# A two-layer transformer on one core: where the softmax maxima of both attentions are split into bf16 parts and turned

## The chip, the core and the metric

The kernel runs on one core of one Trainium2 chip. A core has engines that run side by side, each with its own list of instructions: TensorE (PE in the profile; its weight loads are shown apart, as PEld), VectorE (DVE), ScalarE (ACT), GpSimd (POOL) and SyncE (SP), which issues most of the DMAs. Work reaches TensorE from on-chip SBUF and leaves it in the eight banks of PSUM. Engines wait for each other on semaphores. The metric is the time of one execution on the device in microseconds (us), the median of several; lower is better.

## What is computed

Tokens `x` of shape 8 x 512 x 128 go through four stages, each added to its input: an attention with rotary embedding and a small feed-forward (layer 0), 16 experts of which each token takes two, a causal attention with an extra bias (layer 1), and 8 experts of which each token takes two. The change touches the two attentions. Cut to what matters:

```python
# layer 0, 16 heads of 8 columns
q, k, v = x_norm @ Wq + bq, x_norm @ Wk + bk, x_norm @ Wv + bv
scores = einsum('bhqd,bhkd->bhqk', rope(q) / sqrt(hd), rope(k))
out = softmax(scores) @ v
# layer 1, 16 heads of 8 columns, causal
logits = einsum('bhqd,bhkd->bhqk', q, k) * scale + incidence * decay**(q_pos - k_pos) * bias_scale
attn = softmax(where(causal_mask, -inf, logits))
out = einsum('bhqk,bhkd->bqhd', attn, v)
```

The softmax needs the maximum of each row of logits (one for each token and head) before the exponential is taken.

## The kernel before, in words

**Both attentions** work batch by batch (8 batches of 512 tokens, T = 4 tiles of P = 128 tokens) and in quads of QUAD = 4 heads, so 4 quads a batch and 32 quads in an attention. Each batch of logits is made twice. The first time it stands with the queries on the partitions, so VectorE can take the maximum along a row; the second time it stands transposed, with the keys on the partitions, and there ScalarE takes the exponential. In the transposed form the maximum belongs to a column, so it has to be turned (from 128 tokens x 4 heads to 4 rows x 512 tokens) and subtracted by TensorE as extra rows of the contraction. For that it is held as two bf16 parts, the high part of minus the maximum and what is left.

The step in question, in both attentions, for one quad before the change:

1. VectorE's maxima of the quad are complete (`maxed`; in layer 1 after `join`, L1870, which gives `mjoined`).
2. TensorE: `turn_max` turns the four tiles by fp32 transposes into the PSUM bank `TB` (L1124, L2042).
3. ScalarE: `minus_max` copies `-TB` to bf16, the high part (L808, L1695).
4. VectorE: `minus_max` reads `TB` and the high part and writes the low part (4 rows x 512; L949, L1874). On VectorE's list it stands after further maxima.
5. The two parts reach the product. In layer 0 by two DMAs on SyncE into the rows `STACK` of `QS` (L658, `mstacked`). In layer 1 directly: the matmul of `pick` and `less` (L2049 in `diagonal`, L2054 in `below`) adds them to the scores.
6. `scores(i, g, 0)` of the quad on TensorE waits for `mstacked` (layer 0) or for `mhigh` and `mlow` (layer 1).

**The order on each engine** is written out by hand. In layer 0 a quad has 8 units `j`; in unit `j` TensorE runs `scores(i, g, j)` (L1156), at `j == 5` the `turn_max` of the next quad, then the logits of a head 12 units ahead (L1116), parts of `values` (L1135) and small pieces of other batches. VectorE runs two maxima (L944) per unit, `attend` (L955, L959) at `j == 4`, `minus_max` at `j == 5`.

In layer 1 TensorE runs, for a quad, four times `scores(i, g, j)`, pieces of other batches and `logits` of the next quad's head `j + 1`; then `scores(i, g, 4)`, `values(.., 0)`, `turn_max` of the next quad and `values` 1 to 3, and then the first `scores` of the next quad. `logits` is the product of the incidence (L2016, 54 rows contracted), the diagonal blocks (L2022, L2023) and the blocks of the past (L2028 to L2034). VectorE takes them with `maxima` (L1849, L1854, L1855, L1857, L1862, L1865). Its list at the end of a quad is: `join` of the next quad, `maxima` of one head of the quad after it, `minus_max`, then `attend` of this quad (L1881, L1885), which waits until TensorE has turned the values (L2103). In `scores(i, g, j)` with `j < 4` the products are, in order: L2048 (transposed diagonal), L2049, L2054, L2055, L2048, L2049, L2054, L2055, L2048, L2049; in `scores(i, g, 4)` they are four times L2048, L2049, L2054, L2055.

`less` is 128 rows x 2 x 512 in bf16 before, zero but for rows 0 to 3 (high) and 32 to 35 (low); `pick` is 128 rows x 4 x 128 and selects a head's rows.

In the built program each matmul carries the size of the array tile that it uses: the contracted rows rounded up to 32, 64 or 128, and the columns of the stationary operand likewise. Before, L2016 carries 64 x 128 (54 rows), the products of `values` (L1135, L2093) carry 128 x 32, and nearly all others 128 x 128. A quad takes about 20 us in layer 1 (634 us for 32) and 17.5 us in layer 0 (560 us for 32).

## Time and profile before

| | us |
|---|---|
| median of 3 runs | 1950.77 |
| lowest, highest | 1941.09, 1951.09 |
| profiled execution, its own time | 1956.3 |
| its span, first to last instruction | 1954.6 |
| attention of layer 0, main part | 90 to 650 |
| attention of layer 1, main part | 1032 to 1666 |

Over the whole span PE is busy 77%, DVE 65%, ACT 46%, POOL 35%. The rows that the prediction rests on stand below. In a timeline a row gives the start, the length, the engine, the line, the operation, out<-in with the shapes, how many in a row (x4), and in brackets how long the engine sat idle before it and what ended that. Matmuls overlap: each lasts some 0.2 us, but the next starts well before that, so the price of one is the distance between two starts. A row of several (x2) spans from the first start to the last end.

### The profile page before, as it was taken

Reading aid. Unit: us, or ns where it says so; the run is one execution under the profiler, and the core shown is the slowest. Engines: PE = TensorE matmul, PEld = TensorE weight load, DVE = VectorE, ACT = ScalarE, POOL = GpSimd, SP = SyncE. Lnnn points to the kernel's source line nnn. Section 1 sums busy time; section 2 is a strip of 40 time slices with the busy share of each in tenths; the row PEclk is TensorE's granted clock in tenths of the full one; section 3 lists DMA queues with packets and bytes.
Section 4 is the critical chain, followed back from the end, with each engine's and each line's share of the span. In section 5 each row is a group of like instructions: output and inputs, shape, how many; then the busy total and the mean of one; then the engine's idle time right before and its main releaser. Section 6 shows DMA issues by size and latency. Waiting matters only on the chain. (4 is left out here: it accounts for less than half of the span.)

```text
span 1954.6 us, 37276 instructions
## 1 busy us (share of the span) xinstructions
PE 1498.3 (77%) x11726; PEld 965.0 (49%) x11726; DVE 1274.9 (65%) x3485; ACT 891.8 (46%) x1807; POOL 681.0 (35%) x774
## 2 busy tenths in 40 slices
PE   1699999999999735996248979889798878325993
PEld 0123333333333325996125656666566655224993
DVE  1577888888888413555427777787777775553555
ACT  0156666666666502653334444554445534102661
POOL 1311223323321232553434333343334400475552
PEclk9998999999999957998659999999999999556997
DMA  4211112111111321224052444434444340411225
GB/s 110 65 42 54 38 46 60 47 49 59 47 49 31 118 105 41 72 71 117 27 173 82 133 119 139 119 108 132 121 131 122 111 132 11 127 47 55 72 73 148
DMA packets 121617, 166.36 MB, mean 85 GB/s; under 512 B 21458, under 2 KB 94962, under 8 KB 120786
## 3 DMA queue, kind: packets, MB, share of 16 engines
q1 hardware_dynamic: 112530, 145.69, 26.0%
q0 software_dynamic: 8896, 18.30, 2.7%
q8 instruction: 99, 1.62, 0.4%
q14 instruction: 92, 0.75, 0.1%
HBM read 116.04 MB, written 47.60 MB: 84 GB/s over the span
## 5 line engine op out<-in xcount | busy, mean ns | idle before, releaser
L944 DVE TENSOR_REDUCE a_M<-a_F 128x1 f32<-128x512 f32 x512 | 326.0, 680 | 59.8 <-PE a_F L1116 57.6
L841 ACT ACTIVATE L_W<-a_ST 128x512 f32<-128x512 f32 x512 | 277.2, 595 | 141.4 <-PE a_ST L1156 138.3
L1742 ACT ACTIVATE c_PT<-c_ST 128x1024 f32<-128x1024 f32 x160 | 163.4, 1021 | 201.0 <-PE c_ST L2049 155.3
L1156 PE MATMUL a_ST<-L_W 74*128 74x512 bf16 x512 | 170.8, 397 | 16.7 <-ACT L_W L841 7.2
L1116 PE MATMUL a_F<-L_W 72*128 72x512 bf16 x512 | 168.4, 404 | 13.4 <-DVE a_M L944 13.3
L2048 PE MATMUL c_ST<-ident,c_SD 128*128 128x128 f32 x512 | 145.7, 285 | 25.1 <-issue 17.3
L1135 PE MATMUL a_PV<-L_W,a_V 128*32 128x512 f32 x1024 | 141.1, 625 | 1.0 <-ACT L_W L841 1.0
L2275 ACT ACTIVATE L_hT<-L_P,L_W1s 128x128 f32<-128x128 f32 x316 | 90.6, 369 | 99.0 <-PE L_P L2403 58.3
L1849 DVE TENSOR_TENSOR c_inc<-c_INC,c_table 128x512 f32<-128x512 f32 x128 | 87.5, 684 | 55.5 <-PE c_INC L2016 46.5
L1156 PEld LDWEIGHTS a_ST<-L_W 74*128 74x128 bf16 x512 | 44.6, 99 | 149.4 <-ACT L_W L841 90.7
L2263 POOL DMA_INDIRECT L_yd<-L_ys,L_di x79 | 85.5, 1083 | 91.0 <-DVE L_ys L2348 89.1
L2049 PE MATMUL c_ST<-c_less,c_pick 128*128 128x128 bf16 x512 | 114.0, 223 | 0.0
L2659 ACT ACTIVATE L_hT<-L_P,L_W1s 128x128 f32<-128x128 f32 x284 | 81.4, 369 | 70.6 <-PE L_P L2917 52.3
L2055 PE MATMUL c_ST<-c_QS,c_KS 126*128 126x384 bf16 (+2 forms) x384 | 107.9, 281 | 0.0
L2054 PE MATMUL c_ST<-c_less,c_pick 128*128 128x384 bf16 (+2 forms) x384 | 107.2, 279 | 0.0
L1862 DVE TENSOR_TENSOR c_SD<-c_DIAG,c_inc 128x512 f32<-128x512 f32 x128 | 87.1, 681 | 23.7 <-PE c_ST L2055 23.7
L2022 PE MATMUL c_DIAG<-c_KS,c_QS 72*128 72x128 bf16 x512 | 76.6, 226 | 32.4 <-DVE c_SD L1862 32.4
L2629 POOL DMA_INDIRECT L_yd<-L_ys,L_di x71 | 77.1, 1086 | 68.8 <-DVE L_ys L2822 66.2
L2048 PEld LDWEIGHTS c_ST<-ident,c_SD 128*128 128x128 f32 x512 | 75.2, 147 | 49.5 <-issue 28.0
L439 POOL DMA_INDIRECT L_xd<-L_XN,L_place_i x64 | 62.3, 973 | 100.8 <-issue 87.9
L1116 PEld LDWEIGHTS a_F<-L_W 72*128 72x128 bf16 x512 | 51.4, 101 | 82.7 <-DVE a_M L944 31.1
L1865 DVE TENSOR_REDUCE c_MD<-c_SD 128x4 f32<-128x512 f32 x128 | 88.0, 688 | 4.4
(404 smaller groups left out, 3632.1 us busy)
## 6 DMA issues: line engine op xcount, KB each, us to landing
c_QS<-c_q SPq DMA_DIRECT2D x32, 504.0 KB
c_QS<-c_rd SPq DMA_DIRECT2D x32, 378.0 KB
L_xg<-L_xd SPq DMA_DIRECT2D x150, 64.5 KB
L_W<-a_q SPq DMA_DIRECT2D x32, 288.0 KB
L_W<-a_k SPq DMA_DIRECT2D x96, 96.0 KB
c_KS<-c_k SPq DMA_DIRECT2D x96, 96.0 KB
L_W<-in_L_w SPq DMA_DIRECT2D x8, 1024.0 KB, 12.5
L_got<-L_yd SPq DMA_DIRECT2D x32, 256.0 KB, 4.3
```

What stands on the lines that cost most here:

```text
L841: act.activation(PT[:, j, kk, :], ST[:, kk, :], ACT.Exp).then_inc(sem(exped), 1)
L944: dve.tensor_reduce(M[:, t, h:h + 1], FB[n % BANKS][:, :], AX_X, ALU.max).then_inc(sem(maxed), 1)
L1116: pe.matmul(FB[n % BANKS][:, :], QS[0:STACK, h, t * P:(t + 1) * P], KS[0:STACK, h, :], start=True, stop=True).then_inc(sem(filled), 1)
L1135: last = pe.matmul(PV[32 * j:32 * j + 32, :], V[:, kt, QUAD * g + j, :], PT[:, QUAD * (kt // 2) + j, kt % 2, :], start=(kt == 0), stop=(kt ...
L1156: pe.matmul(ST[:, kk, :], KS[0:KR0, h, kt * P:(kt + 1) * P], QS[0:KR0, h, :], start=True, stop=True).then_inc(sem(scored), 1)
L1742: act.activation(PT[:, j, :, :], ST[:, :, :], ACT.Exp).then_inc(sem(exped), 1)
L1865: dve.tensor_reduce(MD[:, :, h], sd, AX_X, ALU.max).then_inc(sem(maxed), 1)
L2048: pe.matmul(out, SD[:, g % 2, j, t, :], ident[:, :], start=True, stop=False, is_transpose=True)
L2049: return pe.matmul(out, pick[:, j, :], less[:, g % 2, t * P:(t + 1) * P], start=False, stop=True)
L2054: pe.matmul(out, pick[:, j, :], less[:, g % 2, q0:q0 + n], start=True, stop=False)
L2055: return pe.matmul(out, KS[0:KR1, h, kt * P:(kt + 1) * P], QS[0:KR1, h, at:at + n], start=False, stop=True)
L2275: act.activation(hT[:, n % 2, f, :], PS[2 + 2 * (n % 2) + f // 2][:, (f % 2) * P:(f % 2 + 1) * P], func, bias=W1s[:, n % WB, F + f:F + f + ...
```

## The change

VectorE splits the maxima while the tokens still stand on the partitions. It writes `parted` (128 tokens x 4 tiles x 8 columns, bf16): columns 0 to 3 minus the maximum, rounded, columns 4 to 7 what is left. TensorE then turns both parts at once, by four bf16 matmuls with a bf16 identity, into 8 rows x 512; ScalarE copies these to `less` (8 rows), and that is all. VectorE's step on 4 x 512 is gone. In layer 0 both DMAs now wait for the same signal `mset`, and VectorE's split stands at `j == 3`, ahead of `attend`; TensorE's `turn_max` stays at `j == 5`. In layer 1 the split stands right behind `join`, and `turn_max` waits for it. `pick` and `less` shrink from 128 rows to 8, since the low part now lies next to the high one. In the built program L2049 and L2054 (L2053 and L2058 after the change) thereby carry the tile size 32 x 128 in place of 128 x 128, and the four turns 128 x 32, now as plain bf16 matmuls and not as fp32 transposes.

```diff
@@ layer 0
-        mh = sb("mh", [QUAD, 2, S], BF16)
-        ml = sb("ml", [QUAD, 2, S], BF16)
+        parted = sb("parted", [P, T, 2 * QUAD], BF16)
+        less = sb("less", [2 * QUAD, 2, S], BF16)
+        identb = sb("identb", [P, P], BF16)
...
             def stack_max(i, g):
-                for n, (m, part_made) in enumerate(((mh, mhigh), (ml, mlow))):
-                    sp.wait_ge(*turn(part_made, i, g + 1))
-                    sp.dma_start(QS[STACK + n:STACK + n + 1, QUAD * g:QUAD * g + QUAD, :], m[:, g % 2, :]
-                                 ).then_inc(sem(mstacked), 16)
+                sp.wait_ge(*turn(mset, i, g + 1))
+                for n in range(2):
+                    sp.dma_start(QS[STACK + n:STACK + n + 1, QUAD * g:QUAD * g + QUAD, :],
+                                 less[QUAD * n:QUAD * n + QUAD, g % 2, :]).then_inc(sem(mstacked), 16)
...
-                act.activation(mh[:, g % 2, :], TB[0:QUAD, :], ACT.Copy, scale=-1.0).then_inc(sem(mhigh), 1)
+                act.activation(less[:, g % 2, :], TB[0:2 * QUAD, :], ACT.Copy).then_inc(sem(mset), 1)
...
-            def minus_max(i, g):
-
+            def part_max(i, g):
+
+                m = M[:, :, QUAD * g:QUAD * g + QUAD]
+                dve.wait_ge(*turn(maxed, i, QUAD * T * (g + 1)))
+                dve.wait_ge(*turn(mturned, i, g))
+                dve.tensor_scalar(parted[:, :, 0:QUAD], m, -1.0, None, ALU.mult).then_inc(sem(mhigh), 1)
                 dve.wait_ge(*turn(mhigh, i, g + 1))
-                dve.scalar_tensor_tensor(ml[:, g % 2, :], TB[0:QUAD, :], -1.0, mh[:, g % 2, :], ALU.mult,
+                dve.scalar_tensor_tensor(parted[:, :, QUAD:], m, -1.0, parted[:, :, 0:QUAD], ALU.mult,
                                          ALU.subtract).then_inc(sem(mlow), 1)
...
             for n in range(2 * UQ):
                 maximum(0, n)
+            part_max(0, 0)
             for n in range(2 * UQ, 2 * UQ + 2 * AHEAD):
                 maximum(0, n)
-            minus_max(0, 0)
...
-                        if j == 5 and has_quad(g, 1, n1):
-                            minus_max(*next_quad(i, g))
+                        if j == 3 and has_quad(g, 1, n1):
+                            part_max(*next_quad(i, g))
...
             def turn_max(i, g):
-                pe.wait_ge(*turn(maxed, i, QUAD * T * (g + 1)))
+                pe.wait_ge(*turn(mlow, i, g + 1))
 
                 pe.wait_ge(*turn(attn, i, g - 1))
                 for t in range(T):
-                    last = pe.transpose(TB[0:QUAD, t * P:(t + 1) * P], M[:, t, QUAD * g:QUAD * g + QUAD], ident[:, :])
+                    last = pe.matmul(TB[0:2 * QUAD, t * P:(t + 1) * P], parted[:, t, :], identb[:, :],
+                                     start=True, stop=True)
@@ layer 1
-        pick = sb("pick", [P, QUAD, P], BF16)
+        pick = sb("pick", [2 * QUAD, QUAD, P], BF16)
...
-        less = sb("less", [P, 2, S], BF16)
+        parted = sb("parted", [P, T, 2 * QUAD], BF16)
+        less = sb("less", [2 * QUAD, 2, S], BF16)
...
-                act.activation(less[0:QUAD, g % 2, :], TB[0:QUAD, :], ACT.Copy, scale=-1.0).then_inc(sem(mhigh), 1)
+                act.activation(less[:, g % 2, :], TB[0:2 * QUAD, :], ACT.Copy).then_inc(sem(mset), 1)
...
                 dve.tensor_tensor(MD[:, 1:T, hs], MD[:, 1:T, hs], M[:, 1:T, hs], ALU.max).then_inc(sem(mjoined), 1)
-
-            def minus_max(i, g):
+                dve.wait_ge(*turn(mjoined, i, g + 1))
+                dve.wait_ge(*turn(mturned, i, g))
+                dve.tensor_scalar(parted[:, :, 0:QUAD], MD[:, :, hs], -1.0, None, ALU.mult).then_inc(sem(mhigh), 1)
                 dve.wait_ge(*turn(mhigh, i, g + 1))
-                dve.scalar_tensor_tensor(less[LOW:LOW + QUAD, g % 2, :], TB[0:QUAD, :], -1.0, less[0:QUAD, g % 2, :],
-                                         ALU.mult, ALU.subtract).then_inc(sem(mlow), 1)
+                dve.scalar_tensor_tensor(parted[:, :, QUAD:], MD[:, :, hs], -1.0, parted[:, :, 0:QUAD], ALU.mult,
+                                         ALU.subtract).then_inc(sem(mlow), 1)
...
                     if has_quad(g, 2, n1):
                         b, q = next_quad(i, g, 2)
                         maxima(b, QUAD * q)
-                    if has_quad(g, 1, n1):
-                        minus_max(*next_quad(i, g))
...
             def turn_max(i, g):
-                pe.wait_ge(*turn(mjoined, i, g + 1))
+                pe.wait_ge(*turn(mlow, i, g + 1))
...
                 if j == 0:
-                    pe.wait_ge(*turn(mhigh, i, g + 1))
-                    pe.wait_ge(*turn(mlow, i, g + 1))
+                    pe.wait_ge(*turn(mset, i, g + 1))
```

Where the instructions stand in a row. First VectorE in layer 1, from `join` at the end of a quad (L1870 before, L1876 after) to `attend` (L1881 before, L1888 after); L1879 and L1881 of the change are the split. Before:

```order
L1870 TENSOR_TENSOR c_MD<-c_MD,c_M 128x3x4
L1849 TENSOR_TENSOR c_inc<-c_INC,c_table 128x512
L1854 TENSOR_REDUCE c_M<-c_PAST 128x1
L1855 TENSOR_REDUCE c_M<-c_PAST 128x1
L1857 TENSOR_REDUCE c_M<-c_PAST 128x1
L1862 TENSOR_TENSOR c_SD<-c_DIAG,c_inc 128x512
L1865 TENSOR_REDUCE c_MD<-c_SD 128x4
L1874 SCALAR_TENSOR_TENSOR c_less<-c_TB,c_less 4x512
L1881 RECIPROCAL c_rec<-c_TB 128x16
```

And with the change:

```order
L1876 TENSOR_TENSOR c_MD<-c_MD,c_M 128x3x4
L1879 TENSOR_SCALAR c_parted<-c_MD 128x4x4
L1881 SCALAR_TENSOR_TENSOR c_parted<-c_MD,c_parted 128x4x4
L1855 TENSOR_TENSOR c_inc<-c_INC,c_table 128x512
L1860 TENSOR_REDUCE c_M<-c_PAST 128x1
L1861 TENSOR_REDUCE c_M<-c_PAST 128x1
L1863 TENSOR_REDUCE c_M<-c_PAST 128x1
L1868 TENSOR_TENSOR c_SD<-c_DIAG,c_inc 128x512
L1871 TENSOR_REDUCE c_MD<-c_SD 128x4
L1888 RECIPROCAL c_rec<-c_TB 128x16
```

The step that makes the low part has moved from behind one head's maxima to the place right behind `join`, and has become two small instructions.

TensorE at the same place with the change, from the last scores of a quad (L2059) over `values` (L2096) and the turn (L2046) to the first scores of the next; L2053 and L2058 are the products of `pick` and `less`:

```order
L2059 MATMUL c_ST<-c_QS,c_KS 128x128
L2096 MATMUL c_PV<-c_PT,c_V 32x512 x4
L2046 MATMUL c_TB<-c_identb,c_parted 8x128 x4
L2096 MATMUL c_PV<-c_PT,c_V 32x384 x4
L2096 MATMUL c_PV<-c_PT,c_V 32x256 x4
L2096 MATMUL c_PV<-c_PT,c_V 32x128 x4
L2052 MATMUL c_ST<-ident,c_SD 128x128
L2053 MATMUL c_ST<-c_less,c_pick 128x128
L2058 MATMUL c_ST<-c_less,c_pick 128x384
L2059 MATMUL c_ST<-c_QS,c_KS 128x384
```

Nothing has moved here: the same list as before, with 8 turned rows in place of 4, and with the smaller operands in L2053 and L2058.

VectorE in layer 0 at one quad. Before, `attend` (L955, L959) comes first and `minus_max` (L949) after four maxima (L944):

```order
L391 TENSOR_TENSOR L_work<-L_key,L_red 128x64
L955 RECIPROCAL a_rec<-a_TB 128x16
L959 TENSOR_TENSOR a_AT<-a_TB,a_rec 128x4x32
L944 TENSOR_REDUCE a_M<-a_F 128x1 x2
L912 TENSOR_TENSOR a_fresh<-a_PC,a_bv 128x512
L944 TENSOR_REDUCE a_M<-a_F 128x1 x2
L949 SCALAR_TENSOR_TENSOR a_ml<-a_TB,a_mh 4x512
```

With the change:

```order
L953 TENSOR_SCALAR a_parted<-a_M 128x4x4
L955 SCALAR_TENSOR_TENSOR a_parted<-a_M,a_parted 128x4x4
L389 TENSOR_TENSOR L_key<-a_PC,L_br 128x64
L390 TENSOR_REDUCE L_red<-L_key 128x4
L391 TENSOR_TENSOR L_work<-L_key,L_red 128x64
L961 RECIPROCAL a_rec<-a_TB 128x16
L965 TENSOR_TENSOR a_AT<-a_TB,a_rec 128x4x32
L946 TENSOR_REDUCE a_M<-a_F 128x1 x2
L914 TENSOR_TENSOR a_fresh<-a_PC,a_bv 128x512
L946 TENSOR_REDUCE a_M<-a_F 128x1 x4
```

The split now stands ahead of `attend`, and the step after the maxima is gone.

## Rows read from the trace of the kernel before

**Rows 1.** Windows: length; busy PE, PEld, DVE, ACT, POOL; clock; DMA share; GB/s.

```profile
90.00:650.00 560.00, 523.88 (x2818) 202.82 (x2816) 461.95 (x1107) 347.42 (x649) 141.09 (x149) 0.97 0.15 46
1032.00:1666.00 634.00, 545.10 (x5762) 394.30 (x5760) 465.65 (x1060) 307.75 (x434) 204.86 (x250) 0.97 0.38 111
1134.10:1152.80 18.70, 16.55 (x186) 12.19 (x186) 15.57 (x34) 11.96 (x19) 6.84 (x6) 1.00 0.31 90
1177.40:1197.00 19.60, 19.50 (x197) 14.18 (x194) 14.37 (x31) 11.04 (x18) 8.12 (x9) 1.00 0.37 109
```

**Rows 2.** Waits in one batch of layer 1, 1134.1 to 1215.7: total us, times, longest.

```profile
PE c_DIAG L2022 <- DVE c_SD L1862: 4.4, 4, 1.2
PE c_INC L2016 <- issue: 2.7, 1, 2.7
PE c_ST L2048 <- issue: 2.0, 2, 1.6
DVE c_rec L1881 <- PE c_TB L2103: 7.3, 4, 1.8
```

**Rows 3.** Timeline of layer 1, end of a batch's last quad, 1215 to 1221.

```profile
1215.46 0.16 DVE L1870 TENSOR_TENSOR c_MD<-c_MD,c_M 128x12 f32<-128x12 f32 x1
1215.68 0.60 PE L2042 MATMUL c_TB<-ident,c_MD 128*4 128x128 f32 x4 [0.27 <-DVE c_MD L1870]
...
1216.32 0.59 ACT L1695 ACTIVATE c_less<-c_TB 4x512 bf16<-4x512 f32 x1 [0.84 <-PE c_TB L2042]
...
1218.57 0.68 DVE L1874 SCALAR_TENSOR_TENSOR c_less<-c_TB,c_less 4x512 bf16<-4x512 f32 x1
...
1219.35 0.30 PE L2048 MATMUL c_ST<-ident,c_SD 128*128 128x128 f32 x1 [1.64 <-issue]
...
1221.07 0.26 DVE L1881 RECIPROCAL c_rec<-c_TB 128x16 f32<-128x16 f32 x1 [1.82 <-PE c_TB L2103]
```

**Rows 4.** Timeline of layer 1, another end of a quad, 1177 to 1180.

```profile
1177.36 0.60 PE L2042 MATMUL c_TB<-ident,c_MD 128*4 128x128 f32 x4
...
1178.61 0.68 DVE L1874 SCALAR_TENSOR_TENSOR c_less<-c_TB,c_less 4x512 bf16<-4x512 f32 x1 [0.66 <-ACT c_less L1695]
...
1179.37 0.14 PEld L2048 LDWEIGHTS c_ST<-ident,c_SD 128*128 128x128 f32 x1 [0.24 <-issue]
```

**Rows 5.** Timeline of layer 1, the first quad's first scores.

```profile
1036.87 0.45 PE L2048 MATMUL c_ST<-ident,c_SD 128*128 128x128 f32 x1 [3.14 <-issue]
```

**Rows 6.** Timeline of layer 0, its first quad, 90 to 99.

```profile
90.67 4.42 PE L1116 MATMUL a_F<-L_W 72*128 72x512 bf16 x8
...
96.13 0.67 DVE L949 SCALAR_TENSOR_TENSOR a_ml<-a_TB,a_mh 4x512 bf16<-4x512 f32 x1
...
98.58 0.61 PE L1156 MATMUL a_ST<-L_W 74*128 74x512 bf16 x1 [3.50 <-DMA L_W<-a_ml]
```

**Rows 7.** Timeline of TensorE in layer 0, a turn and what follows it.

```profile
361.32 0.60 PE L1124 MATMUL a_TB<-ident,a_M 128*4 128x128 f32 x4
361.76 0.60 PE L1116 MATMUL a_F<-L_W 72*128 72x512 bf16 x2
362.29 0.64 PE L1135 MATMUL a_PV<-L_W,a_V 128*32 128x512 f32 x4
```

**Rows 8.** Timeline of TensorE in layer 1, single matmuls around L2016.

```profile
1200.40 0.27 PE L2103 MATMUL c_TB<-ident,c_pvs 128*128 128x128 f32 x1
1200.61 0.23 PE L2016 MATMUL c_INC<-c_KI,c_QI 54*128 54x128 bf16 x1
...
1200.78 0.22 PE L2016 MATMUL c_INC<-c_KI,c_QI 54*128 54x128 bf16 x1
1200.93 0.23 PE L2022 MATMUL c_DIAG<-c_KS,c_QS 72*128 72x128 bf16 x1
...
1210.60 0.22 PE L2049 MATMUL c_ST<-c_less,c_pick 128*128 128x128 bf16 x1
1210.79 0.21 PE L2016 MATMUL c_INC<-c_KI,c_QI 54*128 54x128 bf16 x1
```

More of the change, by code:

```diff
@@ L874, in _ @@
             dve.memset(V[:, :, :, :], 0.0).then_inc(vmade, 1)
-            dve.wait_ge(vmade, 1)
+            dve.tensor_copy(identb[:, :], ident[:, :]).then_inc(vmade, 1)
+            dve.wait_ge(vmade, 2)
             dve.memset(V[:, :, :, HD:HD + 1], 1.0).then_inc(vmade, 1)
             dve.wait_ge(weights, block_weights)
-            dve.wait_ge(vmade, 2)
+            dve.wait_ge(vmade, 3)
             dve.wait_ge(r_made, r.MADE)
@@ L1035, in _ @@
             pe.wait_ge(weights, block_weights)
-            pe.wait_ge(vmade, 2)
+            pe.wait_ge(vmade, 3)
             pe.wait_ge(r_made, r.MADE)
@@ L1331, in layer1_attention @@
         mjoined, mturned = sig("mjoined", NQ), sig("mturned", NQ)
-        mhigh, mlow = sig("mhigh", NQ), sig("mlow", NQ)
+        mhigh, mlow, mset = sig("mhigh", NQ), sig("mlow", NQ), sig("mset", NQ)
         scored, exped = sig("scored", UQ * NQ, UQ + 1), sig("exped", UQ * NQ)
@@ L1521, in _ @@
             pool.memset(pick[:, :, :], 0.0).then_inc(made, 1)
-            pool.memset(less[:, :, :], 0.0).then_inc(made, 1)
-            pool.wait_ge(made, 7)
+            pool.wait_ge(made, 6)
             pool.affine_select(out=pick[:, :, :], in_=pick[:, :, :], compare_op=ALU.not_equal, fill=1.0,
@@ L1529, in _ @@
                                base=0, pattern=[[-1, P]], channel_multiplier=1).then_inc(made, 1)
-            pool.wait_ge(made, 10)
+            pool.wait_ge(made, 9)
             pool.affine_select(out=pick[:, :, :], in_=pick[:, :, :], compare_op=ALU.not_equal, fill=1.0,
-                               base=-LOW, pattern=[[-1, QUAD], [0, P]], channel_multiplier=1).then_inc(made, 1)
+                               base=-QUAD, pattern=[[-1, QUAD], [0, P]], channel_multiplier=1).then_inc(made, 1)
             pool.wait_ge(weights, 16 * NW)
@@ L1768, in _ @@
             dve.wait_ge(weights, 16 * NW)
-            dve.wait_ge(made, 7)
+            dve.wait_ge(made, 6)
             dve.tensor_scalar(dec[:, 1, :], dec[:, 0, :], -44.0, None, ALU.max).then_inc(table_made, 1)
@@ L1894, in _ @@
             scale(1)
-            dve.wait_ge(made, 12)
+            dve.wait_ge(made, 11)
             for h in range(QUAD):
@@ L2037, in turn_max @@
             def turn_max(i, g):
-                pe.wait_ge(*turn(mjoined, i, g + 1))
+                pe.wait_ge(*turn(mlow, i, g + 1))
                 pe.wait_ge(*turn(attn, i, g - 1))
                 for t in range(T):
-                    last = pe.transpose(TB[0:QUAD, t * P:(t + 1) * P], MD[:, t, QUAD * g:QUAD * g + QUAD],
-                                        ident[:, :])
+                    last = pe.matmul(TB[0:2 * QUAD, t * P:(t + 1) * P], parted[:, t, :], identb[:, :],
+                                     start=True, stop=True)
                 last.then_inc(sem(mturned), 1)
@@ L2110, in _ @@
                     pe.wait_ge(made2, 6)
-            pe.wait_ge(made, 11)
+            pe.wait_ge(made, 10)
             for done in (turn(points, 0, 8), turn(projected, 0, 2), turn(vdone, 0, 1), turn(lraw, 0, 5)):
```

4 lines of the change are left out of this document (1 added, 3 removed).

## The prediction, made before the changed kernel was run

> **What bounds the kernel now.** I read the windows first, then the waits of one batch, then the timeline at the ends of quads. The windows show TensorE as the fullest engine of both attentions: busy 524 of 560 us in layer 0 and 545 of 634 us in layer 1 [rows 1]. In layer 1 the share differs by quad. A batch of it has four ends of quads, which I call A, B, C, D in the order 1134, 1153, 1177 and 1197. Between C and D TensorE is busy 19.5 of 19.6 us, and between A and B 1.6 of its 2.1 idle us are the wait at the start, at A [rows 1, 3]. Between B and C and late between D and A it waits for VectorE, 4.4 us a batch in four waits of up to 1.2 us, and once a batch for transfers, 2.7 us in this one [rows 2]. So an added TensorE microsecond counts in full in A to B and C to D, and partly disappears in the other two stretches.
>
> The second thing to see is what holds the first scores of a quad. At A (the row at 1215) the join ends at 1215.62, the turn starts at 1215.68, ScalarE has the high part at 1216.91, but VectorE takes one head's maxima first and makes the low part from 1218.57 to 1219.25. The scores start at 1219.35, after 1.64 us of idle time, 3.67 us after the turn [rows 3]. At C VectorE is there early, waits for ScalarE, ends at 1179.29, and the scores' weights load at 1179.37, 2.0 us after the turn, with 0.24 us idle [rows 4]. At B the idle time is the other 0.4 us of the 2.0 [rows 2]. VectorE's own next step, `attend`, follows the scores by 1.72 us and has waited 1.82 us by then [rows 3], four times a batch [rows 2]. So both engines start the next quad earlier by what the first scores gain.
>
> **What the change gives.** VectorE loses 0.68 us a quad (the 4 x 512 step) and gets two instructions on 128 x 16. The nearest row is the join, 0.16 us on 128 x 12; with the second one a little longer and the waits between them I take 0.4 us, bounds 0.3 to 0.5. In layer 1 they stand between the join and the turn.
> - At A: join, 0.4, turn. The four turns are 0.06 us apart in place of 0.11, and as `values` on both sides use the same 128 x 32 tile, they no longer force a change of tile: 0.23 us in place of some 0.55. Then ScalarE's 0.59 ends 1.0 us after the turn starts, and the `values`, which took 1.2 us after the turn, end at 1.5. The scores start 1.6 us after the turn, 2.0 after the join, in place of 3.7: 1.7 us gained.
> - At B the `values` wait for the exponential; 0.5 us gained. At C and D the scores come at 1.6 in place of 2.0: 0.4 each.
> - Over layer 1: 7 times A and B, 17 times C, D and the last quads: 7 x 1.7 + 7 x 0.5 + 17 x 0.4 = 22 us. The first quad of layer 1 waits for its low part too, behind sums and a head's maxima, 3.1 us [rows 5]; the 0.4 off and some for VectorE's pace behind it, 2.3 gained.
> - Layer 0: the first scores wait until 98.58 for the transfer of the low part, made at 96.13, while TensorE was free from 95.1 [rows 6]. Both transfers now leave at about 92. Scores start at about 95.5: 3.1 us gained. Later quads don't wait for it.
>
> In the steady part of layer 0 I count nothing. TensorE's turn takes 0.44 us now [rows 7]; bf16 it takes 0.23, and two changes of tile (below) of 0.09 each, 0.41 in all. VectorE saves 0.68 - 0.4 = 0.3 us a quad, but has the 0.4 ahead of `attend`, for which the turn waits in some quads. Bounds -5 to +5 us.
>
> Gains together: 22 + 2.3 + 3.1 = 27 us.
>
> **What the change costs.** The products of `pick` and `less` contract 8 rows and thereby use a 32 x 128 tile, between neighbours that use the whole array. The trace of before has no such tile; it has the 64 x 128 tile of L2016 and the 128 x 32 tile of `values`, and what happens at their borders [rows 8]. Equal bf16 neighbours of 128 columns start 0.06 us apart (the four L2016 from 1200.61 to 1200.78). From the last L2016 (1200.78) to L2022 (1200.93) it is 0.15, so 0.09 more. From the fp32 turn at 1200.40, where the next start is due after 0.11, to L2016 it is 0.21, 0.10 more. From L2049 to L2016 it is 0.19, 0.13 more. In layer 0, two L1116 are 0.22 us apart, and from the second, at 361.98, to L1135 it is 0.31, 0.09 more [rows 7]. Nothing else is waited for in these rows, so a change of tile costs TensorE 0.09 to 0.13 us; I take 0.095. For the 32-row tile the bounds are 0 (no change of tile, or a cheap one) and the whole length of a matmul in these rows, 0.22, less the 0.06 that it takes anyway, 0.16, if the results of one tile must be written before another adds to them in the same PSUM bank.
>
> `scores(i, g, j)` for j below 4 goes in and out three times: 6 changes, 0.57 us. `scores(i, g, 4)` has 8: 0.76 us. A quad has 32 and 3.04 us, all of layer 1 about 990 (some fall together with those of L2016) and 94 us. What of that lies on the path, in one batch:
> - A to B: all 3.0.
> - B to C: with the other two of these waits VectorE paces the second and third head, and the transfers the fourth; scores 0 (0.57) and 4 (0.76) remain: 1.3.
> - C to D: all 3.0.
> - D to A: scores 0 and 1 delay VectorE's list, 1.1; the rest falls into two of the four waits for VectorE and into the wait for the join [rows 2, 3].
>
> 8.5 us a batch, seven times, 60 us; 6 more in the first quad and in the last ones, where VectorE and ScalarE wait more. 66 us. The wait for transfers once a batch (2.7 us in this one) takes up about 0.8 more, since their chain starts only between A and B: 5.6 us off. Cost 60 us.
>
> Here a rule of the Trainium skill is weighed. The trace shows borders of 64-row and 32-column tiles, each dearer by 0.09 to 0.13 us [rows 7, 8], and none of a 32-row tile. The Trainium skill, page "TensorEngine Tiling (Array Packing)", section "Tiling Modes", says that changing the tiling mode, and not merely the tile, drains TensorE; it gives no price. By it, with the price of the rows, the sum is the one of the forecast. The page "TensorE: Matmul & The Clock Gate", section "Why this matters for your kernels", says that a single matmul over 32 rows takes the same time as one over 128; taken alone it puts the whole cost at nothing, and the time would be that of the first rival.
>
> **Sum.** +60 - 27 = +33 us. The profiled execution took 1956.3 us (1954.6 of span) and would become 1989; against the median of 1950.77 the forecast is 1984 us.
>
> **Rivals.**
> 1. *Small tiles cost nothing*, and only the gains are left. For it: rows of few contracted rows last no longer than full ones (54 rows 0.22 to 0.23 us, 128 rows 0.22 [rows 8]). Against it: the four borders above. 1950.8 - 27 = 1924 us, faster. It decides below a price of about 0.04 us a change, where 27 us of gains meet the cost on the path (about 630 changes' worth).
> 2. *The dearer border.* Products of one accumulation now stand on both sides of a change: L2048 opens a bank's columns by the whole array and L2049 adds to them from the small tile. If that waits for the write, a change costs 0.16: 66 x 0.16 / 0.095 = 111, less 5.6 and 27: +78, 2029 us. The borders in the rows have no such pair.
> 3. *The idle time of TensorE takes most of it.* TensorE is idle for 89 of 634 us in layer 1 [rows 1], and 94 us are added. If VectorE's and the transfers' pace holds more stretches than I gave them, half of the 60 goes: 1954, no change. Against it: 19.5 busy of 19.6 us from C to D.
>
> **Chances.** Forecast 0.71, with a range of its own of 1962 to 2015 (price 0.08 to 0.13, steady layer 0 by 5 either way). Rival 1: 0.13. Rival 2: 0.08. Rival 3: 0.08. The range 1945 to 2035 leaves out rival 1 and some of the far end. A measurement of this kernel can tell about 0.5% from no change, so 1941 to 1960.5 is the same. Slower: 0.71, 0.08 and a part of rival 3, less the forecast's low end, 0.77; same 0.09; faster 0.14.
>
> **What would show it.** In the changed profile: single L2053 start 0.2 us after L2052 in place of 0.11, and L2059 0.15 after the end of L2058's columns; weight loads of L2053 and L2059 are no longer ahead of their matmul. `scores` with j = 0 to 3 takes 0.5 to 0.6 us longer. C to D is 19.6 + 2.6 us; at A the wait of 1.64 us is gone and the join-to-scores distance is 2.0 us. VectorE's busy time falls by about 64 x 0.3 = 18 us, and its two new instructions take under 0.25 us each. The scores of layer 0 start at 95.5. I am wrong if the starts of L2052 and L2053 stay 0.11 us apart (rival 1), or if layer 0 moves by more than 5 us beyond its first quad.

## The result, and the profile after

| | median us | runs from, to | profiled execution | TensorE busy us | VectorE busy us |
|---|---|---|---|---|---|
| before | 1948.93 | 1941.09 to 1951.09 | 1956.3 | 1498.3 | 1274.9 |
| after | 2011.19 | 2005.84 to 2012.38 | 2005.84 | 1597.0 | 1273.1 |

The changed kernel is slower: ratio 1.033, interval 1.0307 to 1.0354, which is 62 us (6 runs of each). The forecast was 33 us slower, in a range that holds 2011. The direction and the main mechanism (the price of a change of tile) came out; the forecast size was half of what was measured. The experiments below show where the rest is.

The page of the changed kernel, busy time by engine over the span:

```profile
PE 1597.0 (80%) x11726; PEld 946.1 (47%) x11726; DVE 1273.1 (64%) x3550; ACT 892.0 (45%) x1807; POOL 680.0 (34%) x773
```

TensorE runs the same 11726 matmuls and is busy 99 us longer. The windows of the changed kernel show where, in the columns of [rows 1]: layer 0, layer 1, and then five stretches of layer 1, each from one turn of the maxima to the next (from the start of ScalarE's copy of `TB` to that of the next): A to B, B to C, C to D, D to A, and B to C of a later batch.

```profile
90.00:650.00 560.00, 521.11 (x2785) 198.18 (x2786) 456.86 (x1131) 341.68 (x638) 139.03 (x147) 0.96 0.15 46
1030.00:1700.00 670.00, 634.29 (x5698) 376.71 (x5697) 469.92 (x1097) 306.22 (x431) 204.75 (x251) 0.95 0.37 107
1226.58:1245.93 19.35, 19.35 (x194) 11.71 (x186) 16.85 (x35) 13.51 (x21) 8.18 (x8) 1.00 0.34 98
1245.93:1269.59 23.66, 20.37 (x176) 11.41 (x176) 15.12 (x43) 9.82 (x14) 7.05 (x8) 0.93 0.46 135
1269.59:1291.95 22.36, 22.36 (x196) 13.51 (x192) 14.08 (x32) 10.94 (x18) 8.61 (x9) 1.00 0.29 86
1291.95:1312.02 20.07, 19.20 (x192) 12.13 (x188) 15.62 (x39) 7.41 (x9) 6.57 (x14) 1.00 0.50 149
1508.91:1535.51 26.60, 22.66 (x176) 12.19 (x176) 15.40 (x43) 9.82 (x15) 7.04 (x8) 0.82 0.46 125
```

Layer 1 went from 545 busy us to 634, and two of its four stretches are now filled to the last hundredth. The borders, that is the places where a matmul on one tile size follows one on another, can be seen one by one. Timeline of TensorE inside one `scores`, first in the kernel before and then in the changed kernel:

```profile
1202.68 0.27 PE L2048 MATMUL c_ST<-ident,c_SD 128*128 128x128 f32 x1
1202.79 0.22 PE L2049 MATMUL c_ST<-c_less,c_pick 128*128 128x128 bf16 x1
1202.85 0.27 PE L2054 MATMUL c_ST<-c_less,c_pick 128*128 128x256 bf16 x1
1202.96 0.27 PE L2055 MATMUL c_ST<-c_QS,c_KS 126*128 126x256 bf16 x1
```

```profile
1333.07 0.27 PE L2052 MATMUL c_ST<-ident,c_SD 128*128 128x128 f32 x1
1333.28 0.23 PE L2053 MATMUL c_ST<-c_less,c_pick 8*128 8x128 bf16 x1
1333.34 0.27 PE L2058 MATMUL c_ST<-c_less,c_pick 8*128 8x256 bf16 x1
1333.54 0.28 PE L2059 MATMUL c_ST<-c_QS,c_KS 126*128 126x256 bf16 x1
1333.66 0.27 PE L2052 MATMUL c_ST<-ident,c_SD 128*128 128x128 f32 x1
```

From L2052 to L2053 it is 0.21 us (0.11 in the kernel before); L2053 to L2058, both on the 8 rows, 0.06; L2058 to L2059 0.20 for 256 columns (0.11 before). Over all of layer 1, where the clock is full, the medians say the same: 0.207 against 0.112 us on the way in, 0.200 against 0.108 on the way out, and 0.067 against 0.056 between two small tiles. So 0.10 us on the way in, 0.09 on the way out, and next to nothing in between. The matmuls last what they did; their distances grew.

The gain of the new way is there as well. The place that answers to [rows 3], in the changed kernel (it is the end of a batch's first quad, here and there, and not of its last as the heading of [rows 3] says: ScalarE's copy is the tenth of 32, and serves quad 1 of the third batch):

```profile
1225.52 0.16 DVE L1876 TENSOR_TENSOR c_MD<-c_MD,c_M 128x12 f32<-128x12 f32 x1
1225.72 0.17 DVE L1879 TENSOR_SCALAR c_parted<-c_MD 128x16 bf16<-128x16 f32 x1
1225.93 0.18 DVE L1881 SCALAR_TENSOR_TENSOR c_parted<-c_MD,c_parted 128x16 bf16<-128x16 f32 x1
...
1226.58 0.59 ACT L1701 ACTIVATE c_less<-c_TB 8x512 bf16<-8x512 f32 x1 [0.23 <-PE c_TB L2046]
...
1227.77 0.14 PEld L2052 LDWEIGHTS c_ST<-ident,c_SD 128*128 128x128 f32 x1 [0.20 <-issue]
1227.77 0.33 PE L2052 MATMUL c_ST<-ident,c_SD 128*128 128x128 f32 x1
```

Join at 1225.52, scores at 1227.77: 2.25 us in place of 3.89. TensorE's 1.64 idle us ahead of these scores are gone; only its weight load shows 0.20. And in layer 0 the first scores start at 95.35 (98.58 in [rows 6]).

What I hadn't expected stands in layer 0. In five of the eight batches the changed kernel has this (timeline of GpSimd, VectorE and TensorE):

```profile
314.86 1.15 POOL L711 TENSOR_TENSOR a_part<-a_rot,a_part 128x512 bf16<-128x512 f32 x1 [3.41 <-ACT a_part L803]
314.94 1.10 DVE L953 TENSOR_SCALAR a_parted<-a_M 128x16 bf16<-128x16 f32 x1
316.08 0.18 DVE L955 SCALAR_TENSOR_TENSOR a_parted<-a_M,a_parted 128x16 bf16<-128x16 f32 x1
316.17 0.22 DVE L389 TENSOR_TENSOR L_key<-a_PC,L_br 128x64 f32<-128x64 f32 x1
316.44 1.16 PE L1069 MATMUL a_PC<-a_W,YT 128*128 128x128 f32 x8 [1.29 <-DVE L_key L389]
```

The split's first instruction, whose median over the 32 quads is 0.196 us, takes 1.10 here. It started 0.08 us after GpSimd's L711 and ended 0.03 us after it. Behind it stands the routing's `choose` (L389), which frees the PSUM bank `PC`, and TensorE waits 1.29 us for that, five times 1.3 or 6.5 us in all. In the kernel before nothing stood ahead of `choose` there, and none of these five waits exists.

### The profile page after: what moved, and what is told of

Read it like the earlier page. It is cut to its first block and busy times, and to the rows that moved or that the text cites. A ratio compares the mean times of both kernels' runs of the same rounds, so it can differ in the third digit from the quotient of the medians.

```text
span 2004.1 us, 37408 instructions
## 1 busy us (share of the span) xinstructions
PE 1597.0 (80%) x11726; PEld 946.1 (47%) x11726; DVE 1273.1 (64%) x3550; ACT 892.0 (45%) x1807; POOL 680.0 (34%) x773
## 5 line engine op out<-in xcount | busy, mean ns | idle before, releaser
L2052 PE MATMUL c_ST<-ident,c_SD 128*128 128x128 f32 x512 | 149.3, 292 | 5.0 <-ACT c_PT L1748 5.0
L2053 PE MATMUL c_ST<-c_less,c_pick 8*128 8x128 bf16 x512 | 117.1, 229 | 0.0
L2059 PE MATMUL c_ST<-c_QS,c_KS 126*128 126x384 bf16 (+2 forms) x384 | 111.0, 289 | 0.0
L2058 PE MATMUL c_ST<-c_less,c_pick 8*128 8x384 bf16 (+2 forms) x384 | 106.2, 277 | 0.0
L2096 PE MATMUL c_PV<-c_PT,c_V 128*32 128x512 f32 (+3 forms) x1024 | 94.0, 481 | 0.1
L2053 PEld LDWEIGHTS c_ST<-c_less,c_pick 8*128 8x128 bf16 x512 | 46.8, 91 | 95.7 <-issue 74.6
```

The lines of the kernel that those rows point to most:

```text
L2052: pe.matmul(out, SD[:, g % 2, j, t, :], ident[:, :], start=True, stop=False, is_transpose=True)
L2053: return pe.matmul(out, pick[:, j, :], less[:, g % 2, t * P:(t + 1) * P], start=False, stop=True)
L2058: pe.matmul(out, pick[:, j, :], less[:, g % 2, q0:q0 + n], start=True, stop=False)
L2059: return pe.matmul(out, KS[0:KR1, h, kt * P:(kt + 1) * P], QS[0:KR1, h, at:at + n], start=False, stop=True)
L2096: last = pe.matmul(PV[32 * j:32 * j + 32, kt * P:S], V[:, kt, QUAD * g + j, :], src, start=(kt == 0), stop=(kt == T - 1), skip_group_check ...
```

## The experiments

The ratios are each against the kernel before on the same chip. Chips differ: in the first four runs the kernel before took 1944.6 us, in the others 1993 to 1995; so ratios are compared, not times, and 1 % is about 19.5 us. "Turn to turn" is always the distance between the starts of ScalarE's copies of `TB`.

**1. The new way without small tiles.** Layer 1's `less` and `pick` keep 128 rows, with zeros (the fill of `less` with zeros is left out here):

```diff
-        pick = sb("pick", [2 * QUAD, QUAD, P], BF16)
-        less = sb("less", [2 * QUAD, 2, S], BF16)
+        pick = sb("pick", [P, QUAD, P], BF16)
+        less = sb("less", [P, 2, S], BF16)
...
-                act.activation(less[:, g % 2, :], TB[0:2 * QUAD, :], ACT.Copy)
+                act.activation(less[0:2 * QUAD, g % 2, :], TB[0:2 * QUAD, :], ACT.Copy)
```

> The changed kernel, but in layer 1 pick and less have 128 rows again (rows 8 to 127 zero), so that all products of the scores use the whole array; split, turn and waits stay as changed. Theory (the cost is the borders of the 32-row tile, 0.10 us into it and 0.09 out of it in the changed kernel's trace): only the gains are left, 1949 - 25 = 1924 us, with up to 10 more if layer 0's own loss, seen in the trace, stays. Rival (the cost comes from the split ahead of the turn, or from TensorE's clock, which was at half speed longer in the changed kernel for a reason of its own): stays above 1985 us.

Measured: 1932.26 us, ratio 0.9923 (0.9889 to 0.9957). The loss turned into a gain of 12 us by the medians, 15 by the ratio, so 79 us of the changed kernel (1.033 less 0.992) go with the 8-row tiles. But the gain is only about half of my 27.

**2. The borders without the new way.** The kernel before, its products cut to rows 0 to 63, which hold both parts:

```diff
-                return pe.matmul(out, pick[:, j, :], less[:, g % 2, t * P:(t + 1) * P], start=False, stop=True)
+                return pe.matmul(out, pick[0:64, j, :], less[0:64, g % 2, t * P:(t + 1) * P], start=False, stop=True)
...
-                pe.matmul(out, pick[:, j, :], less[:, g % 2, q0:q0 + n], start=True, stop=False)
+                pe.matmul(out, pick[0:64, j, :], less[0:64, g % 2, q0:q0 + n], start=True, stop=False)
```

> The kernel before, but in layer 1 the products of pick and less contract rows 0 to 63 alone (the low part lies in rows 32 to 35), which gives them a 64 x 128 tile; nothing else differs. Theory: the same number of borders at the same price and none of the gains, 1949 + 62 + 25 = 2036 us (2015 to 2045). Rival (only a 32-row tile, or the other parts of the change, cost anything): 1945 to 1955 us.

Measured: 2019.08, ratio 1.0366 (1.0312 to 1.0421), 74 us slower by the medians and 71 by the ratio; 2036 was expected. So two edited lines in the kernel before cost more than the whole change. The tile of 64 rows costs at its borders what that of 32 does: medians of 0.207 us in, 0.202 out and 0.066 between two of them.

**3. Layer 1's part alone** (layer 0 as before).

> Layer 1 as changed, layer 0 as before. By the two traces layer 0 ends 6 us later with the change, though its first quad gains 9; theory: 2011 - 6 = 2005 us. Rival (my forecast, that layer 0 gains 3 us by its first quad and nothing else): 2014 us.

Measured: 1998.22, ratio 1.0253 (1.0206 to 1.03). The changed kernel is 0.8 % above it. The intervals don't meet, so layer 0's part, for which I had counted a gain of 3 us, costs.

**4. Is it the turn's narrow tile in layer 0?** As 1, with `parted` of layer 0 padded to 128 columns, so that its turn uses the whole array:

```diff
-        parted = sb("parted", [P, T, 2 * QUAD], BF16)
+        parted = sb("parted", [P, T, P], BF16)
...
-                    last = pe.matmul(TB[0:2 * QUAD, t * P:(t + 1) * P], parted[:, t, :], identb[:, :],
+                    last = pe.matmul(TB[:, t * P:(t + 1) * P], parted[:, t, :], identb[:, :],
```

> As e1, and in layer 0 the part tile is padded with zeros to 128 columns, so that its four bf16 turns use the whole array and not a 128 x 32 tile. If the borders of that small tile are what layer 0 loses by: 32 quads x 0.18 = 6 us below e1. If it is the place of the split ahead of attend, or the clock: within 3 us of e1.

Measured: 1929.9, ratio 0.99 (0.9864 to 0.9936); the intervals of 1 and 4 overlap for the most part. By the times a gain of 2 us, or of the 6 expected, is not told apart from none. The trace decides: from turn to turn a steady batch of layer 0 begins with 18.63 us here and 18.66 in kernel 1, where the kernel before has 17.3. The narrow tile is not what lengthens that stretch.

**5 and 6. Which quads pay?** As 1, but the 8 rows back in two quads of four:

```diff
+                rows = 2 * QUAD if g in (1, 3) else P
-                pe.matmul(out, pick[:, j, :], less[:, g % 2, q0:q0 + n], start=True, stop=False)
+                pe.matmul(out, pick[0:rows, j, :], less[0:rows, g % 2, q0:q0 + n], start=True, stop=False)
```

(the same in `diagonal`; `(0, 2)` in the other run).

> e1_full_rows (128 rows) but the 8-row products back in quads 1 and 3 of layer 1 alone, that is in the stretches A to B and C to D. By the terms of my sum (3.0 us a batch in each): 48 us above e1_full_rows, ratio to before 1.017. By the turn-to-turn times of the changed kernel against e1_full_rows (1.6 and 3.7 us): 40 to 42 us, ratio 1.013. If part of the cost came from the clock alone after a transfer wait in B to C: clearly less, under 30 us.

> e1_full_rows but the 8-row products in quads 0 and 2 of layer 1 alone, the stretches D to A and B to C. By the terms of my sum (1.1 and 1.3 us a batch): 19 us above e1_full_rows, ratio to before 1.002. By the turn-to-turn times of the changed kernel against e1_full_rows (1.3 and about 4 us): 38 to 42 us, ratio 1.013: then B to C, where the transfer wait and the half clock are, is the stretch that the sum undersized.

Measured: 1.0152 (1.0116 to 1.0188) and 1.0121 (1.0081 to 1.0161), against 0.9923: 45 and 39 us. Together 84, against 79 for all four quads at once. Quads 0 and 2, which I had at 19 us, cost twice that; quads 1 and 3, which I had at 48, a little less. Turn to turn in the middle batches, in us:

| stretch | before | 1: whole array | 5: quads 1, 3 | 6: quads 0, 2 | after |
|---|---|---|---|---|---|
| D to A | 18.7 | 18.8 | 18.8 | 20.1, twice 21.6 | 20.1 |
| A to B | 19.6 | 17.8 | 19.35 | 17.8, twice 19.2 | 19.35 |
| B to C | 22.0 to 25.4 | 20.5 to 24.2 | 21.1 to 24.7 | 25.2 to 25.4 | 23.5 to 26.7 |
| C to D | 19.4 | 18.9 | 22.4 | 18.9 | 22.4 to 22.7 |

Where the granted clock is 1.00, the prices stay in the stretch whose quad has small tiles, and repeat to a tenth. The two exceptions of run 6 follow each other, D to A at a granted clock of 0.91 and A to B at 0.93. Windows of kernel 1 (A to B, B to C of a later batch, C to D, D to A) show what each met:

```profile
1214.34:1232.11 17.77, 16.68 (x194) 12.43 (x186) 16.85 (x35) 13.39 (x21) 8.17 (x8) 1.00 0.35 103
1387.76:1410.80 23.04, 17.21 (x172) 12.26 (x176) 14.89 (x43) 9.70 (x15) 6.98 (x8) 0.93 0.50 137
1256.32:1275.24 18.92, 18.92 (x196) 14.44 (x192) 14.03 (x32) 10.93 (x17) 7.86 (x8) 1.00 0.35 99
1275.24:1294.00 18.76, 16.09 (x192) 12.80 (x188) 15.62 (x39) 7.42 (x10) 7.32 (x15) 1.00 0.54 159
```

C to D has no idle time: 18.92 becomes 22.36, the whole price, 3.44 us for 32 changes, 0.107 each. A to B has 1.1 idle us, and of 2.67 busy us added 1.6 lengthen it. D to A has 2.7 idle, and of 3.1 added 1.3 show. B to C at the same granted clock, 0.93, is 23.66 against 23.04 with 3.2 busy us more: 0.6 in this pair. (Other batches of kernel 1, at 0.92, take 20.5 to 22.6, so a price of up to 3 can't be excluded by it.) But in three of the changed kernel's batches it is 26.6, and these have a lower granted clock. The wait for transfers in the later B to C of above, and windows inside that stretch (the trace names nothing that ends this wait; in the program the instruction stands behind waits for the transfers of `iced` and `stacked`):

```profile
1526.18 0.58 PE L2020 MATMUL c_INC<-c_KI,c_QI 54*128 54x128 bf16 x4 [1.95 <-issue]
```

```profile
1521.00:1524.00 3.00, 3.00 (x20) 1.40 (x16) 2.91 (x7) 1.39 (x2) 0.00 (x0) 1.00 0.65 150
1524.00:1526.00 2.00, 0.23 (x1) 0.00 (x0) 0.35 (x2) 1.55 (x3) 0.31 (x1) 0.95 0.72 194
1526.00:1528.00 2.00, 1.82 (x17) 1.66 (x18) 0.69 (x1) 0.00 (x0) 0.84 (x1) 0.50 0.54 127
...
1534.00:1536.00 2.00, 2.00 (x20) 1.01 (x16) 0.69 (x1) 0.75 (x2) 0.00 (x0) 0.50 0.41 108
1536.00:1538.00 2.00, 2.00 (x26) 1.13 (x18) 0.00 (x0) 0.69 (x2) 0.00 (x0) 0.99 0.72 209
```

TensorE waits 1.95 us, and comes back at half speed (1.2 in place of 2.4 GHz), busy all the time, for 10 us. In the batch at 1245 the half speed is over in 3.4 us, as the granted clock of its windows adds up, after a wait of 1.30:

```profile
1262.00:1264.00 2.00, 1.44 (x16) 1.37 (x17) 0.69 (x1) 0.63 (x1) 1.16 (x1) 0.75 0.60 164
1264.00:1266.00 2.00, 2.00 (x7) 0.95 (x5) 1.09 (x3) 0.00 (x0) 0.00 (x0) 0.50 0.55 147
1266.00:1268.00 2.00, 2.00 (x16) 0.89 (x14) 0.00 (x0) 1.32 (x2) 0.24 (x1) 0.90 0.50 154
```

The length of the wait alone doesn't decide it: in kernel 1 a wait of 2.81 us in B to C (at 1404) goes with a mean of 0.93, and in run 5 one of 2.76 (at 1387) with 1.00. Over seven batches B to C takes 176.8 us in the changed kernel and 156.8 in kernel 1; at 0.6 a batch the border would be 4 of these 20. In run 6 this stretch has a granted clock of 0.73, and the wait for transfers is not what the half speed follows. The whole stretch, and windows inside it:

```profile
1196.52:1221.83 25.31, 24.24 (x172) 13.58 (x176) 15.09 (x43) 9.82 (x15) 7.04 (x8) 0.73 0.45 128
1200.00:1203.00 3.00, 2.96 (x31) 1.75 (x28) 2.92 (x15) 0.94 (x3) 2.24 (x4) 1.00 0.25 66
1203.00:1206.00 3.00, 2.13 (x17) 1.72 (x17) 2.96 (x8) 0.69 (x1) 0.83 (x1) 0.63 0.37 113
...
1218.00:1221.00 3.00, 3.00 (x26) 1.33 (x25) 1.03 (x4) 1.69 (x3) 1.22 (x2) 1.00 0.36 113
```

It begins beside a wait of 0.91 us for VectorE (until 1203.87), lasts 13.7 us, and by then TensorE is so late that it doesn't wait for the transfers at all; the same in six of the batches.

Added up over the seven B to C (twice the stretch times what its granted clock lacks of 1), TensorE ran at half speed for 31 us in the kernel before and in kernel 1, 34 in run 5, 57 in the changed kernel, 71 in run 3 and 93 in run 6. So the longer spells go with small tiles in this very stretch: run 5, whose small tiles stand in two others, stays with the kernels that have none. Why they do is not shown; and run 6, with 93 us of it, takes 176.4 us for the seven, no more than the changed kernel with 57, so a spell's length is not simply its price. Over layer 1 the mean granted clock fell from 0.97 in the kernel before to 0.95, and is 0.97 in kernel 1.

**7. Layer 1's new way, without small tiles, and layer 0 as before.**

> Layer 0 as in the kernel before; layer 1 as changed but with less and pick of 128 rows, so without small tiles. Theory (the layers add: layer 1's part gains 27.6 us between its first and last turn, of which e1_full_rows gave 8 to 9 back by a later start out of layer 0): 20 to 23 us faster than before, ratio 0.988 to 0.990. Rival (layer 0's loss is taken up by waits at the start of layer 1 anyway, so that removing it gives nothing): 12 to 15 us, ratio 0.992 to 0.994 as in e1_full_rows.

Measured: 0.9891 (0.9862 to 0.992), 21 us faster: the lowest ratio of all kernels here, though its interval meets those of 1 and 4. Layer 1's gain is about what I had summed for it, 22 + 2.3. Kernel 1, which differs in layer 0 alone, stands 6 us above it (0.9923).

**8. What does the split wait for in layer 0?** As 1, but the first part by an instruction of another kind, the minus moved to ScalarE's copy:

```diff
-                dve.tensor_scalar(parted[:, :, 0:QUAD], m, -1.0, None, ALU.mult)
+                dve.tensor_reduce(parted[:, :, 0:QUAD], m.rearrange("p t (j o) -> p t j o", o=1), AX_X, ALU.max)
...
-                dve.scalar_tensor_tensor(parted[:, :, QUAD:], m, -1.0, parted[:, :, 0:QUAD], ALU.mult,
+                dve.scalar_tensor_tensor(parted[:, :, QUAD:], m, 1.0, parted[:, :, 0:QUAD], ALU.mult,
```

> e1_full_rows with layer 0's split placed as in the change, but its first part made by a TENSOR_REDUCE over one element (a copy, rounded to bf16) instead of the TENSOR_SCALAR, and the minus moved to ScalarE's copy. Theory (what waits is VectorE's access behind GpSimd's instruction, and the form decides): the first instruction takes about 0.2 us at all 32 places, but then the second one (L955, a SCALAR_TENSOR_TENSOR that reads two tensors in SBUF, 0.175 us at every place so far) takes 0.9 to 1.0 us once a batch, beside the GpSimd instruction, and the time stays that of e1_full_rows within 5 us. The Trainium skill (SBUF - State Buffer, on the shared port pair) says that a reduce never contends with GpSimd and that an instruction with two SBUF inputs does. Rival (TENSOR_SCALAR stretches for a reason of its own): both parts take 0.2 us everywhere and the time falls by 8 to 10 us. Second rival (whatever stands first there waits): the TENSOR_REDUCE itself shows 1.1 us once a batch.

Measured, one execution: 1988.3 against 1995.3, which is 8 us above run 11 on the same chip and not within the 5 expected; one execution settles no time. What decides here are the rows: all 32 quads, minimum/median/maximum in ns, first of the changed kernel and then of this one (L953 in both), and this one's rows beside GpSimd.

```profile
L953 DVE TENSOR_SCALAR a_parted<-a_M x32: 174/196/1103, 90.2 to 652.9; 128x16 bf16<-128x16 f32 x32
```

```profile
L953 DVE TENSOR_REDUCE a_parted<-a_M x32: 169/170/171, 90.3 to 686.3; 128x16 bf16<-128x16 f32 x32
```

```profile
239.86 1.15 POOL L711 TENSOR_TENSOR a_part<-a_rot,a_part 128x512 bf16<-128x512 f32 x1 [3.40 <-ACT a_part L803]
```

```profile
239.93 0.17 DVE L953 TENSOR_REDUCE a_parted<-a_M 128x16 bf16<-128x16 f32 x1
240.14 0.90 DVE L955 SCALAR_TENSOR_TENSOR a_parted<-a_M,a_parted 128x16 bf16<-128x16 f32 x1
240.96 0.21 DVE L389 TENSOR_TENSOR L_key<-a_PC,L_br 128x64 f32<-128x64 f32 x1
```

The reduce passes beside GpSimd in 0.17 us. The next instruction, 0.18 us in the changed kernel at every place, now waits in its stead, in five batches as before, and ends at 241.04, 0.03 after GpSimd. So neither the instruction nor its place among VectorE's is slow; which of them can run beside GpSimd depends on its form. The Trainium skill says this, page "SBUF — State Buffer", section "Who interferes with whom": an instruction of VectorE that reads two tensors in SBUF contends with a GpSimd instruction that reads SBUF, `tensor_scalar` can take the shared port pair too, a reduce never does, and the loser is blocked for the whole instruction. These rows agree: 0.90 us for the instruction with two tensors, 1.10 for `tensor_scalar`, 0.17 for the reduce.

**9, 10 and 11. The split behind `choose`.** As 1, with the split moved behind `choose` in VectorE's list of layer 0:

```diff
-                        if j == 3 and has_quad(g, 1, n1):
-                            part_max(*next_quad(i, g))
...
                             r.choose(dve, i - 2, CHOICES[u], PC)
+                        if j == 3 and has_quad(g, 1, n1):
+                            part_max(*next_quad(i, g))
```

> The change with whole-array borders in layer 1 (its less and pick tensors of 128 rows, as in e1_full_rows), and in layer 0 the split put behind the routing's choose instead of ahead of it. In the changed kernel the split's first instruction (L953, usually 0.17 to 0.20 us) lasts 1.10 us once a batch, beside a GpSimd TENSOR_TENSOR of 1.15 us that began 0.08 us before it; choose's first instruction comes 1.3 us later, and TensorE waits 1.29 us for it (L1069 <- L389). Theory (VectorE stands behind GpSimd there and hands the delay to choose and TensorE): the 1.3 us per batch go, some 8 to 10 us in eight batches, ratio to the kernel before 0.987 against 0.992 with whole-array borders alone, turn-to-turn in that stretch of layer 0 back from 18.66 to 17.3 us. Rival (layer 0's 9 us come from the clock's short dips and not from this wait): 0.992 again.

Measured: 0.9924 (0.9896 to 0.9953), level with 1, where 0.987 was expected. But TensorE's five waits for `choose` are gone and the stretches did move, so the same kernel ran again beside kernel 1:

> The kernel of e9_split_after_choose once more. On its chip a transfer wait of 6 to 8 us a batch stood at the end of layer 0's batch (DVE a_XC L932 <- remote 6.6 us in the kernel with layer 0 as before), in the fourth turn-to-turn stretch, which took 25 to 26 us where it had taken 19.1 to 19.4; what is won ahead of such a wait can be lost in it. Theory: where that wait is absent, the two stretches that came back (18.66 to 17.41 and 18.5 to 17.5 us) are worth 8 to 16 us, ratio to before 0.984 to 0.988. Rival: the ratio is again that of whole-array borders alone, 0.992.

> The kernel of e1_full_rows once more, on the same chip as e10_after_choose_again, so that the two are compared side by side. Both theories: 0.990 to 0.994. It stands 8 to 16 us above e10 by the theory, level with it by the rival.

Measured: 0.9909 (0.9883 to 0.9935) for the moved split and 0.9926 (0.9899 to 0.9954) for kernel 1: 1976.1 against 1980.6 us. The intervals overlap, so 4 us is a leaning and no finding. Turn to turn in layer 0, in one batch (from 307 or 308 on):

| | 1st | 2nd | 3rd | 4th |
|---|---|---|---|---|
| 11: split ahead of `choose` | 18.7 | 18.5 | 19.4 | 25.5 |
| 10: split behind `choose` | 17.4 | 17.5 | 21.0 | 26.3 |
| 7: layer 0 as before | 17.4 | 17.2 | 19.6 | 24.9 |

The first stretch is cured, as the theory wants (17.3 to 17.4 in the kernel before), and the second with it. The third gives most of it back. Windows of that third stretch, first kernel 10, then kernel 11:

```profile
343.24:364.30 21.06, 19.77 (x98) 6.54 (x101) 17.68 (x58) 12.64 (x24) 5.08 (x7) 0.92 0.10 31
```

```profile
344.65:364.04 19.39, 18.07 (x98) 6.22 (x100) 17.25 (x57) 12.57 (x24) 4.74 (x6) 1.00 0.11 33
```

The same work at a granted clock of 0.92 in place of 1.00: 1.7 us more. The fourth stretch has on these chips a long wait (7.2 us of VectorE ahead of L934 in both kernels; 3.1 to 3.7 in the first traces, where the kernel before took 19.1 us for the stretch; the trace doesn't name what ends it), and in it 0.8 us more goes. So the wait behind GpSimd is shown, and that it delayed `choose` and TensorE by 1.3 us in five batches; its removal was worth 0 us in the first comparison and 4 in the second, neither told apart from nothing.

**12. Layer 0's part alone** (layer 1 as before).

> The change in layer 0 alone, layer 1 as in the kernel before. By the terms of my sum (3.1 us gained at the first quad, the rest nil): 3 us faster, ratio 0.998. By the turn-to-turn times of the changed kernel (3 to 4 us gained at the first quad and in the clock's first dip, then 2.2 to 2.8 us lost per batch, the last turn 7 to 9 us late): 5 to 10 us slower, ratio 1.003 to 1.005; if the chip shows the long transfer wait at the end of each batch of layer 0, part of the loss hides in it and it may come out near 1.002.

Measured: 1.0066 (1.0041 to 1.0091), 13 us slower, above both of my figures, though the interval reaches the second one. With run 3 the parts add: 0.66 + 2.53 = 3.19 %, against 3.30 % for the whole. Kernels 1 and 7 put layer 0's part at 6 us, with intervals wide enough for 13.

## Why the prediction was half right

| term | forecast us | measured us | from |
|---|---|---|---|
| small tiles of layer 1 | +60 | +71 (+71, +79) | ratios of runs 3 less 7 (2; after less 1) |
| layer 1's shorter way | -24 | -21 | run 7 |
| layer 0 | -3 | +13 (+15, +6) | run 12 (after less 3; 1 less 7) |
| sum | +33 | +63 | 62 measured |

**Right.** A change of tile costs 0.09 to 0.11 us, as the borders of the 64-row and 32-column tiles in [rows 7, 8] said, and not 0 (rival 1) or 0.16 (rival 2). The faster kernel that rival 1 had in mind exists only without the small tiles, as kernel 1. The gain at A is there (TensorE's 1.64 idle us are gone), and so is the gain of layer 0's first quad (95.35, forecast 95.5). C to D, forecast 22.2, is 22.4. The Trainium skill, page "TensorEngine Tiling (Array Packing)", section "Tiling Modes", has the rule that a change of tiling mode drains TensorE; the distances agree in that every change costs time (0.207 us in place of 0.112), and they don't show what TensorE does in it. The Trainium skill, page "TensorE: Matmul & The Clock Gate", section "Why this matters for your kernels", says that 32 rows take the time of 128; that holds for each matmul (0.23 and 0.22 us), and would have misled without the first.

**The step on the B to C stretch failed.** It was to pay 1.3 us a batch. In the one pair of batches with an equal clock it pays 0.6, but over seven batches it pays 20 us, where I had 9, less 5.6 for cover in the very same wait. I had carried every term at the clock of the batch that I read. The spells at half speed in this stretch are longer with small tiles, up to 10 us in place of 3.4 (13.7 in run 6), and the added time is not covered by the wait for transfers.

**The step on A to B was wrong by nearly as much, the other way.** I had "all 3.0" on the path, since the only large wait there would go. It pays 1.6: kernel 1 still has 1.1 idle us in that stretch, most of them waits of 0.37 and 0.75 us for ScalarE's exponential, and these take up the rest. C to D pays 3.4 to 3.8 (3.0), D to A 1.3 (1.1). So a steady batch pays 9.3 us where my four terms add up to 8.4 (I wrote 8.5), and that the cost of layer 1 came so near, 60 against 71, is partly luck: +1.6 in B to C and -1.4 in A to B cancel.

**The step "in the steady part of layer 0 I count nothing" failed.** It gave bounds of -5 to +5 us, and it was some 16 (13, and the 3 that the first quad gained; 9 by kernels 1 and 7). My own sign of being wrong, layer 0 moving by more than 5 us beyond its first quad, came true. I had priced the split at 0.4 us from the join, whose row shows it with GpSimd idle; the two instructions take 0.35 to 0.37 us in the median and so the term was right where nothing interferes, but in five batches they take 1.3 us. A row of the kernel before could have warned me, the same place of layer 0 on GpSimd and VectorE:

```profile
323.11 1.16 POOL L710 TENSOR_TENSOR a_part<-a_rot,a_part 128x512 bf16<-128x512 f32 x1 [3.40 <-ACT a_part L802]
```

```profile
323.31 0.22 DVE L390 TENSOR_REDUCE L_red<-L_key 128x4 f32<-128x64 f32 x1
323.57 0.77 DVE L391 TENSOR_TENSOR L_work<-L_key,L_red 128x64 f32<-128x64 f32 x1
```

L391 takes 0.23 us in the changed kernel; here it ends at 324.34, when GpSimd has ended at 324.27. But it stood behind L389, which alone TensorE waits for. And I had looked at what stands behind the split for `attend` only, not for `choose`, which TensorE waits for in the quad where both stand at `j == 3`. Of the 13 us, five times 1.3 or 6.5 are seen in this way. A steady batch loses 2.8 us in all (73.2 to 76.0 turn to turn), and the rest stands mostly in the second stretch (18.5 in place of 17.2 in most batches). The clock is as large a term: from 250 to 650 its mean is 0.99 in the kernel before and 0.96 in the changed kernel, and on the other chips 0.94 in run 7 and 0.91 in run 12. Against these stand the first quad's gain and a shorter first spell at half speed (6.8 us in place of 20.5). How they divide is not settled, and what lowers the clock is not shown: in run 10, with the waits behind GpSimd gone, it is 0.92.

**Also off:** VectorE's busy time was to fall by 18 us and fell by 1.8. The step on 4 x 512 saved 43 us; the two new ones took 34, not 26, and most of the other 7 is the join, which was not changed: it never took over 0.172 us before and takes 1.11 once a batch after (in seven of them), beside a GpSimd instruction that it now meets (and so does the split of layer 1 right behind it, 1.08 us; TensorE does not wait for it there).
